# Fusing norm and projections of a second attention layer, and stacking its heads on four 32-row groups

## The reference

```python
h = layernorm(x)                                   # no gain, no bias, eps 1e-5
q = rope((h @ wq).reshape(4, 1024, 16, 8))
lat = h @ w_down                                   # 128 -> 64
k = rope((lat @ wk_up).reshape(4, 1024, 16, 8))    # 64 -> 128
v = (lat @ wv_up).reshape(4, 1024, 16, 8)
scores = einsum('bqhd,bkhd->bhqk', q, k) / sqrt(8)
allowed = (arange(1024) // 32)[None, :] <= (arange(1024) // 32)[:, None]
attn = softmax(where(allowed, scores, lowest))
x = x + einsum('bhqk,bkhd->bqhd', attn, v).reshape(4, 1024, 128) @ wo
```

## Time and profile before

| | us |
|---|---|
| median of three runs | 2290.97 (2288.64 to 2308.19) |
| profiled execution, its own time | 2288.33 |
| its span | 2286.5 |
| norm stage of layer two (1177.3 to 1217.0) | 39.7 |
| projection stage (to 1337.9) | 120.9 |
| attention stage (to 1902.9) | 565.0 |
| output projection (to 1926.4) | 23.5 |
| second experts (to the end) | 360.1 |

### The profile page before, as it was taken

How to read it: one execution, slowest core, us unless ns; L and a number is a source line. 1 busy time by engine, 2 the same in 40 slices (tenths; PEclk the granted TensorE clock), 3 DMA queues, 4 the chain that set the end, 5 groups by cost and what they waited for, 6 DMA issues and landing times. The chain is left out here.

```text
span 2286.5 us, 39722 instructions
## 1 busy us (share of the span) xinstructions
PE 1803.5 (79%) x11252; PEld 1116.8 (49%) x11300; DVE 1413.4 (62%) x2718; ACT 1200.5 (53%) x1688; POOL 496.7 (22%) x804
## 2 busy tenths in 40 slices
PE   1599999999999999742835719999899994474993
PEld 1366666666666666432832303333333333344993
DVE  4267677766676777641554448788788863522665
ACT  1478778787787777411622203556566662221441
POOL 0112211121122111105410011122122222074441
PEclk9999999999999999955966657999999997586996
DMA  4656666665566666141224541322233202511224
GB/s 168 149 143 151 157 155 156 158 146 144 143 150 157 156 156 153 40 95 49 60 63 177 176 134 32 62 52 48 54 61 61 48 15 96 72 55 49 60 61 129
DMA packets 158933, 239.46 MB, mean 105 GB/s; under 512 B 21691, under 2 KB 107932, under 8 KB 158205
## 3 DMA queue, kind: packets, MB, share of 16 engines
q1 hardware_dynamic: 148102, 222.90, 39.9%
q0 software_dynamic: 6592, 13.56, 1.8%
q10 hardware_dynamic: 4160, 2.10, 0.3%
HBM read 87.18 MB, written 50.17 MB: 60 GB/s over the span
## 5 line engine op out<-in xcount | busy, mean ns | idle before, releaser
L1012 ACT ACTIVATE a_p<-a_score 128x1024 f32<-128x1024 f32 (+3 forms) x384 | 300.7, 810 | 244.4 <-PE a_score L1029 240.4
L1118 DVE TENSOR_REDUCE a_mx<-a_misc 128x1 f32<-128x512 f32 (+3 forms) x768 | 376.3, 548 | 77.8 <-PE a_misc L1060 51.5
L438 ACT ACTIVATE a_p<-a_score 128x1024 f32<-128x1024 f32 (+3 forms) x384 | 290.4, 809 | 182.7 <-PE a_score L464 179.5
L1057 PE MATMUL a_misc<-a_k,a_q 72*128 72x512 bf16 (+3 forms) x768 | 251.7, 349 | 80.8 <-DMA a_v<-values 55.4
L464 PE MATMUL a_score<-a_q,a_kh 128*128 128x512 f32 (+3 forms) x768 | 274.9, 369 | 22.8 <-DMA a_q<-a_stage 19.4
L480 PE MATMUL a_out<-a_p,a_v 128*64 128x512 f32 (+3 forms) x1536 | 290.7, 500 | 0.0
L395 POOL TENSOR_SCALAR_AFFINE_SELECT a_p<-a_p 128x256 f32<-128x256 f32 x256 | 124.0, 514 | 719.4 <-ACT a_p L451 719.4
L451 ACT ACTIVATE a_p<-a_p 128x2560 f32<-128x2560 f32 (+1 forms) x128 | 274.6, 2145 | 1.1
L464 PE MATMUL a_score<-a_q,a_kl 128*128 128x512 f32 (+3 forms) x768 | 254.8, 348 | 0.0
L610 DVE TENSOR_TENSOR a_part<-a_part,a_p 128x1024 f32<-128x1024 f32 (+3 forms) x256 | 224.0, 875 | 8.4 <-ACT a_p L451 1.8
L1029 PE MATMUL a_score<-a_q,a_k 128*128 128x512 bf16 (+3 forms) x720 | 216.0, 327 | 1.9 <-ACT a_p L1012 1.3
(11 more groups left out here) (205 smaller groups left out, 2834.7 us busy)
## 6 DMA issues: line engine op xcount, KB each, us to landing
a_kh<-a_stage SPq DMA_DIRECT2D x128, 256.0 KB, 4.2
a_kl<-a_stage SPq DMA_DIRECT2D x128, 256.0 KB, 4.8
a_q<-a_stage SPq DMA_DIRECT2D x128, 256.0 KB, 5.5
a_xt<-xt SPq DMA_DIRECT2D x32, 512.0 KB
a_q<-qk_parts SPq DMA_DIRECT2D x144, 64.0 KB
a_k<-qk_parts SPq DMA_DIRECT2D x144, 64.0 KB
values<-p_v SPq DMA_DIRECT2D x16, 512.0 KB, 5.3
a_v<-values SPq DMA_DIRECT2D x16, 512.0 KB
```

The costliest lines, as they stand in the source:

```text
L438: nc.scalar.activation(chunk_of(prob[p], c), score_ps[:, c % 2, :, 0:width], ACT.Tanh, scale=scale / clamp).then_inc(tanh_done, 1)
L1012: nc.scalar.activation(prob[s % RING][:, :, 0:width], score_ps[:, s % 2, :, 0:width], ACT.Exp, scale=scale).then_inc(exp_done, 1)
L1057: mm = nc.tensor.matmul(misc[:, bank, 0:keys], q_st[bn][0:ROWS, h, t * P:(t + 1) * P], k_st[bn][0:ROWS, h, key0:key0 + keys], start=True, ...
L1118: nc.vector.tensor_reduce(m[c][:, h, t:t + 1], misc[:, bank, 0:keys], AX_X, ALU.max).then_inc(free, 1)
```

## The change

The norm and projection stages become one, `norm_project1`. It reads x from SBUF. Sequence by sequence it computes statistics and the normed tiles on DVE, turns them on PE, copies them out on ACT and makes latent, q, values and k. q and k are made in halves of 512 tokens, each half of plain and of partner in a PSUM bank of its own. The latent is made twice, on partitions 0 to 63 and 64 to 127, so that k's plain product reads one copy and its partner the other; the values are made from both copies in turn. The split is into two fp32r parts (`PARTS = 2`), high by ACT and low by POOL, and three of their products are used.

The operands are laid out in DRAM as attention wants them (`qk_stack`): each head has 32 rows, 24 for the products, 2 for the negated maximum, 3 for the page mask and the rest unused, so that four heads fill 128 partitions. The three kinds of stores write 21 MB in place of 14.7 (stack 16.8, values 4.2). POOL's queue stores the fixed rows, SP's the parts and values. The buffers and the semaphores of the stores live on in `Projected`, and attention waits for them before it loads.

In attention a unit is loaded by two DMAs for q and k and one for the values. A matmul for scores or maxima runs on 26 rows of one row group, on 29 (with the mask rows) where it makes a diagonal block; diagonal blocks are matmuls of their own, so there are 72 for scores and 72 for maxima per unit, and the mask is in the products. POOL has no work. The maxima have a wide region of two banks, reduced for two heads at once (14 reduces per unit), and a narrow one of a single bank (12 reduces, and all transposes); the order of the two is written out in `early_jobs` and `rest_jobs`. The ring has 8 places, and values products come in pairs of chunks, after slots 3, 7, ... 23. The negated maxima go into q's buffer by four DMAs. The heads' output is kept by quad, divided with one instruction per half, and gathered by the copies of `project_out1`.

```diff
-PARTS = 3
-V_COLS = 32
+PARTS = 2
+PRODUCTS = ((0, 0), (0, 1), (1, 0))
+MAX_ROW = len(PRODUCTS) * DH1
+MASK_ROW, MASKS = MAX_ROW + PARTS, P // PAGE - 1
+STACK = 32
+V_COLS = 16
...
+def norm_project1(nc, kit, sem, x, ident, eps, wq_dram, wdown_dram, wk_dram, wv_dram, rope_dram, stack_dram, v_dram, kept):
...
             def _(sp):
...
+                        rows = stack_dram[b, i].rearrange("g (h r) t -> (g h) r t", r=STACK)
+                        for what in range(PARTS):
+                            sp.wait_ge((hi_done, lo_done)[what], 2 * b + i + 1)
+                            for n, product in enumerate(PRODUCTS):
+                                if product[i] == what:
+                                    sp.dma_start(rows[:, n * DH1:(n + 1) * DH1, :], part[i][b % 2][:, what, :].bitcast(F32))\
+                                        .then_inc(kept.stored[b], 16)
...
+            @block.gpsimd
+            def _(pool):
...
+                        pool.dma_start(rows[MAX_ROW:STACK], fixed[i][:].to_broadcast([STACK - MAX_ROW, HEADS1, SEQ]))\
+                            .then_inc(kept.fixed_stored, 16)
...
+                turn(0)
+                for b in range(BATCH):
+                    latent(b)
+                    rotated(b, 0)
+                    value(b)
+                    if b + 1 < BATCH:
+                        turn(b + 1)
+                    rotated(b, 1)
...
+                def high(b, i):
+                    act.wait_ge(rot_done, nth(b, i, 1) + 1)
+                    if b >= 2:
+                        act.wait_ge(kept.stored[b - 2], 16 * kept.STORES)
+                    nc.scalar.copy(part[i][b % 2][:, 0, :], rot[i][:]).then_inc(hi_done, 1)
...
+    wide_jobs = [job for pieces in ([(0, 3, 0)], [(2, 4, 0)], [(2, 5, 0)], [(2, 6, 0)], [(2, 7, 0)], [(1, 7, 1)],
+                                    [(0, 1, 0), (1, 5, 1)]) for job in jobs(WIDE, pieces)]
+    narrow_jobs = [job for pieces in ([(0, 0, 0), (1, 4, 1)], [(0, 2, 0)], [(1, 6, 1)]) for job in jobs(NARROW, pieces)]
+    W, N = iter(wide_jobs), iter(narrow_jobs)
+    early_jobs = [next(W if k == "w" else N) for k in "wwnwwnn"]
+    rest_jobs = [next(W if k == "w" else N) for k in "wnwnwnwnwwnwnwnwnwn"]
...
+        def load_rows(sp, n, b3):
...
+            kit.ge_apart(sp, scored, (n - BUFS + 1) * SLOTS)
...
+        def load_values(sp, n, b3):
...
+            kit.ge_apart(sp, pv_pairs, (n - BUFS + 1) * ROUNDS)
...
-        def pool_step(pool, u, b3, d3):
...
-            for h in range(QUAD):
-                slot = (2 * i + h // 2) % RING
-                mm = nc.tensor.matmul(out_ps[h * V_COLS:(h + 1) * V_COLS, HALF - width:HALF],
-                                      v_st[b3][:, j, h, :], prob[slot][:, h % 2, 0:width],
-                                      start=j == 0, stop=j == last_j)
-            mm.then_inc(pv_chunks, 1)
+            diagonal = P if j // (TILES // 2) == half else 0
+            for a, b, last_row in ((0, diagonal, MASK_ROW + MASKS), (diagonal, width, MASK_ROW)):
+                if a == b:
+                    continue
+                for h2 in range(2):
+                    row = STACK * (2 * hp + h2)
+                    mm = nc.tensor.matmul(score_ps[:, s % 2, h2, a:b], k_st[b3][row:row + last_row, j * P:(j + 1) * P],
+                                          q_st[b3][row:row + last_row, q0 + a:q0 + b], start=True, stop=True)
+            mm.then_inc(scored, 1)
+
+        def pe_pv(pe, m, b3, pair, loads):
...
+            pe.wait_ge(exp_done, m * SLOTS + 4 * pair + 4)
+            for i in (2 * pair, 2 * pair + 1):
...
-            ge(pe, free, number if isinstance(u, int) and at < BANKS else number - (BANKS - 1))
+            back = back_to_same_region(u, at)
+            if back is not None:
+                ge(pe, free, number - (back - 1))
...
-                if diagonal:
-                    mm = nc.tensor.matmul(misc[:, bank, keys - P:keys], identb[:], page_mask[:],
-                                          start=False, stop=True)
...
+                banks = narrow_ps[:].unsqueeze(1) if region == NARROW else wide_ps[:]
+                frm = banks[:, :, 0:len(pieces) * keys].rearrange("p h (n k) -> p h n k", k=keys)
...
+                nc.vector.tensor_reduce(to, frm, AX_X, ALU.max).then_inc(free, 1)
...
+                sp.wait_ge(kept.fixed_stored, 16 * kept.FIXED_STORES)
+                sp.wait_ge(kept.stored[0], 16 * kept.STORES)
+                for i in range(2):
+                    load_rows(sp, i, i)
+                    load_values(sp, i, i)
+                for b in range(1, BATCH):
+                    sp.wait_ge(kept.stored[b], 16 * kept.STORES)
...
-NEGATIVE = -3e38
+NEGATIVE = -2.0 ** 73
...
-                    nc.vector.tensor_copy(here[:], hflat[:, bass.ds(nxt * SEQ, SEQ)]).then_inc(staged, 1)
+                    nc.vector.tensor_copy(by_tile, heads[:, :, bass.ds(nxt * TILES, TILES), :]).then_inc(staged, 1)
...
+            in_stage(norm_project1, x, ident, eps, wq, w_down, wk_up, wv_up, rope, stack, values, kept)
+            heads = inner.sb("heads", [P, QUADS, ALL_TILES, QUAD * DH1])
+            in_stage(attention1, stack, values, kept, heads, ident, DH1 ** -0.5)
+            nc.clear_and_free_semaphores(kept.all_semaphores())
+            nc.all_engine_barrier()
```

More of the change, by code:

```diff
@@ L737, in project1 @@
[L737 to L744, removed]
@@ L745, in project1 @@
[L745 to L747 removed]
+        stats = [k.sb(f"p1_stats{i}", [P, TILES, 6]) for i in range(2)]
+        mv = [k.sb(f"p1_mv{i}", [P, TILES, 2]) for i in range(2)]
+        std = [k.sb(f"p1_std{i}", [P, TILES]) for i in range(2)]
@@ new lines, in norm_project1 @@
+        partner = k.ps("p1_partner", [P, 2, HALF])
+        part, values, fixed = kept.part, kept.values, kept.fixed
+        w_loaded, rope_loaded, v_set, fixed_made = (sem(f"p1_{n}") for n in ("w_loaded", "rope_loaded", "v_set", "fixed_made"))
+        stats_done, mv_done, std_done, rstd_done, xn_done = (sem(f"p1_{n}") for n in ("stats", "mv", "std", "rstd", "xn"))
+        turn_done, xt_done, lat_done, lat_out, v_done, v_out = \
+            (sem(f"p1_{n}") for n in ("turn", "xt", "lat", "lat_out", "v", "v_out"))
@@ L780, in _, with turn @@
             @block.tensor
             def _(pe):
[L782 to L787, removed]
+                def turn(b):
+                    pe.wait_ge(xn_done, TILES * (b + 1))
+                    ge(pe, xt_done, b)
+                    for t in range(TILES):
+                        mm = nc.tensor.transpose(turned[:, t * P:(t + 1) * P], xn[b % 2][:, t, :], ident[:])
+                    mm.then_inc(turn_done, 1)
@@ new lines, in value @@
+                def value(b):
+                    pe.wait_ge(lat_out, b + 1)
+                    for t in range(TILES // 2):
+                        for half in range(2):
+                            tile = half * (TILES // 2) + t
+                            rows = slice(half * L, (half + 1) * L)
+                            mm = nc.tensor.matmul(lat_ps[:, tile * P:(tile + 1) * P], lat[b % 2][rows, tile * P:(tile + 1) * P],
+                                                  wv[rows, :], start=True, stop=True)
+                    mm.then_inc(v_done, 1)
@@ L818, in _ @@
                     act.wait_ge(v_done, b + 1)
[L819 to L825, removed]
@@ L866, in attention1 @@
+                statistics(0)
+                normed(0)
+                statistics(1)
+                dve.wait_ge(rope_loaded, 16)
+                for b in range(BATCH):
+                    if b + 1 < BATCH:
+                        normed(b + 1)
+                    rotate(b, 0)
+                    if b + 2 < BATCH:
+                        statistics(b + 2)
+                    rotate(b, 1)
+def attention1(nc, kit, sem, stack_dram, v_dram, kept, out, ident, scale):
     UNITS = BATCH * QUADS
-    ROWS = PARTS * PARTS * DH1
```

527 lines of the change are left out of this document (278 added, 249 removed).

## The result

| | before | after |
|---|---|---|
| median, us | 2293.8 (4 runs, 2288.6 to 2308.2) | 2426.5 (4 runs, 2424.0 to 2429.1) |
| ratio | | 1.057, 95% interval 1.052 to 1.062 |
| span of the profiled execution | 2286.5 | 2427.4 |
| norm and projections | 160.6 | 140.6 |
| head of attention, to the first negated maxima | 50.4 | 46.1 |

The change costs 5.7%, where 1.3% was forecast. By stages, against the earlier trace rows: -20.0, -4.3, +141.8, +19.0; with +3.6 ahead of the change and +0.8 behind it that is the difference of the spans, 140.9.

What follows compares the result with a forecast made beforehand. The prediction took PE to bound attention's intervals, DVE next, and no engine the norm and projection stages. 2286.5 - 80 - 10 + 117 + 3 = 2316.5 in the profile, +4.5 gives 2321 us; range 2200 to 2415.

Steps and rivals of the forecast that it cites:

- Projections: Norm and projection stage: fused into a pipeline over four sequences, 81 us instead of 160.6, a gain of 80.
- both of its bounds: Projection stage's 21 MB of stores: 52 us at 407 GB/s, or 73 us at 288 GB/s, still within 81.
- The third rival: Projections: fixed rows read from 8 partitions hold up the queues, 20 us less gain, 2341 in all; chance small.
- Head: Start of attention, to the first negated maxima: 40 us instead of 50.4, a gain of 10 (bounds 0 and 15).
- The reading: PE in attention: the clock follows the rows in use, so it swings and a unit takes 40 us; chance 0.5.
- clearly under 0.98: Sign that the forecast is right: granted clock over attention's 15 intervals below this, with an interval near 40 us.
- The first rival: Attention: the clock holds at 2.4 GHz, a unit takes 33.7 us, 2226 in all, faster by 3%; chance 0.3.
- A unit: Attention's 15 intervals: 40 us each instead of 32.2, the middle of 33.7 and 46.2, 117 us lost.
- the walk: Slot-by-slot estimate of an attention unit's 24 slots with one wide region: 33.7 us at 2.4 GHz, 46.2 at 1.2.
- The sum of PE's work one after another, 31.8: Attention unit at 2.4 GHz without overlap: scores 10.4, maxima 10.4, values 9.4, transposes 1.1, changes 0.5 us.
- the 33.7 of the walk: Attention unit at full clock with heads overlapping: 18.8 us in 9 cycle-bound intervals plus 14.9 in 5 PE-bound ones.
- Tail: Last unit of attention, without maxima: stays at 31.6 us, as PE at 1.2 GHz needs 18.9 + 10 + 1.

Runs made afterwards that it cites:

- the stage alone: Kernel before with only the fused norm and projection stage, three bf16 parts, no fixed rows, attention compute untouched: 2214.0 us, again over four runs 2218.3 us, ratio 0.966.
- the run on 32 rows: Kernel before with scores and maxima over rows 0 to 31 only, instead of 128 and 72 rows: 2745.9 us.
- the run on 128 rows: Changed kernel with every matmul of scores and maxima over all 128 rows, so the attention is not computed: 2357.2 us.
- the run on 128 rows with short reduces: Changed kernel with scores and maxima over all 128 rows, and each reduce of the maxima reading only 64 columns per block: 2274.8 us.

## Why the prediction was wrong

The direction was right and the size was not: 2426.5 against a range to 2415. With the fixed rows read from DRAM the same kernel took 2354.5, inside the range, so the next term alone put it outside.

**Projections, the term that failed.** I put them at 81 and they took 140.6. The fused stage is as long as forecast where the fixed rows don't hold it up, 76.1 and 80.3, but that is partly luck. The 81 had PE busy for 15.5 per sequence, 62 in all, and DVE for 48. With the stage alone PE was busy 44.4 us and DVE 58.8: it is DVE that comes nearest to bounding it. The failed step is "Such rows went at 407 GB/s, which gives 52 us, under the compute": it took the rate of stores from 128 partitions for stores from 8, and both of its bounds (407 and 288) came from rows of the wrong kind. The third rival named the mechanism and gave it 20 us and a small chance; it was worth 64 in the stage and 5 in the head. From 1180 to 1330 the fixed rows held the DMA engines for 71 us and SP's transfers for 63, together 134, near the stage's 140.6; the prediction had 52 for both, since it had the fixed rows at 407 GB/s, and 4.2 MB in 71 us are 59. Inside the stage this shows as the wait of ACT for the first sequence's buffer, 62.3 us: the same kind of wait that the change had removed.

The Trainium skill has this (SBUF — State Buffer, section "Door 1: The DMA port swizzle"): a transfer's rate depends on how many of 16 ports its partitions reach. By its mapping partitions 0 to 7 reach two ports, which it puts at some 27 GB/s each, so an estimate of 54. The runs agree: 52 from POOL's queue, 51 from ACT's.

**Head.** 40 was forecast and 46.1 measured; 41.0 where the stores were quick. The first loads stood behind late stores: PE's first maxima began 12.6 us into the head, and 7.6 where the stores were quick.

**The clock.** The reading held: granted clock 0.62, "clearly under 0.98", with rises behind the value pairs. The run on 32 rows shows it in a stretch without gaps, and the run on 128 rows shows the reverse. The first rival (the clock holds) is out. The Trainium skill (TensorE: Matmul & The Clock Gate, section "HAM oscillation") speaks of idle gaps only; in the run on 32 rows PE had none and stayed at 1.2 GHz, so the measurement decides against it as the only cause.

**A unit.** 40 was forecast, 41.7 measured, so the 15 intervals missed by 25 of 142. That is near, but the account behind it was incomplete. The wide region was named and is worth 4 of the 5 us of the reduces. The pairs of value chunks were in the walk only as work of PE; as a block during which DVE and ACT run idle, they cost 4.4 us that no step of mine had. With single chunks ACT's waits for scores fell from 381 to 313 us in the 15 intervals, and DVE's for the turned maxima and outputs from 86 to 14. The sum of PE's work one after another, 31.8, was good: PE was busy 32.1 per unit in the run on 128 rows with short reduces. Full overlap of heads and full clock together was not reached by any run, so the 33.7 of the walk stays untested.

**Tail.** "31.6 stays, since PE at 1.2 GHz needs 18.9 + 10 + 1" was wrong by 19: a sum of PE's work where PE and ACT take turns. PE's timeline in the tail of the kernel after:

```profile
2013.82 3.19 PE L1166 MATMUL a_out<-a_p,a_v 128*16 128x512 f32 x16
2016.93 0.80 PE L1151 MATMUL a_score<-a_q,a_k 26*128 26x512 f32 x4
2018.91 1.71 PE L1151 MATMUL a_score<-a_q,a_k 26*128 26x512 f32 x4 [1.17 <-ACT a_p L1130]
2020.54 1.48 PE L1166 MATMUL a_out<-a_p,a_v 128*16 128x256 f32 x16
```

During the 3.2 us of a pair ACT runs dry, and then PE waits 1.2 for ACT. The tail was 50.6, 42.6 on 128 rows, and 38.8 with single chunks as well. Of the remaining 7.2 us over 31.6, some 2 are not a loss: the last negated maxima now leave earlier in their unit, so 33 exponentials lie in the tail where there were 31, and 31.6 us for 31 are 1.0 each (an estimate). The other 5 are open.

**Sum.** Of the 105.5 us between 2321 and 2426.5, 60 are the projections, 25 the intervals, 19 the tail, 6 the head and 1 the rest (4.4 for the 3 forecast, of which 3.6 lie ahead of the change and are no part of it); against them, the median lies 0.9 below the profiled span where I had put it 4.5 above.

## What to carry to other kernels

Count the partitions that a DMA reads or writes before its bytes: a small constant replicated from a few partitions can hold up every other transfer, and the buffers behind it. Before matmuls are packed onto few rows, ask what else in the stretch works on all rows, since the engine may lose its clock and with it more than the packing gives. And where two engines take turns over a small buffer, walk the turns: a sum of one engine's work is only a lower bound.

## What the hardware showed

- PE, busy 922 of 924.5 us with scores and maxima on 32 rows and values on 128, was granted 1.2 GHz throughout; the same matmuls on 72 and 128 rows had 0.98 of 2.4 GHz.
- Stores from 8 partitions ran at 48 to 55 GB/s from a software and a hardware queue alike. The software queue kept the DMA engines at a busy share above 0.9 meanwhile, the hardware queue at 0.48.
- Matmuls in two groups of 64 rows started within 0.01 us of each other, and a pair of 512 columns in fp32 advanced PE by 0.43 us, from 1299.82 to 1300.25.
- Issuing those eight stores held ACT for 30.05 us, and POOL for 4.81.
